# Two more waits in GpSimd's loop: a product behind an output sum, a coupling behind a division

## Chip, cores and metric

The kernel runs on one core of a Trainium2 chip. The metric is device time in microseconds of one execution, taken as the median of several runs. The engines of the core are PE (TensorE, matrix products), DVE (VectorE), ACT (ScalarE), POOL (GpSimd) and SP (SyncE, which issues the transfers). Each runs its own list of instructions in order, and they meet in semaphores: an instruction that finishes raises a counter, and another engine waits until that counter has reached a value.

## What is computed

A decoder layer over 64 independent sequences of 256 tokens and 256 features. It is a state-space mixer, a cross-attention from the mixed tokens to a context of 120 tokens plus the tokens themselves, and a "coupled" feed-forward of three cycles, each followed by a residual layer norm.

```python
x = layernorm(x + mixer(x))            # SSD with chunks: C, B, decay matrix Lmat, x * dt
x = layernorm(x + xattn(ctx, x))       # 8 heads of 64, softmax over 120 + 256 keys
x = layernorm(x + ffn(x))

# mixer, the part that matters here
Y_diag = einsum('bclhn,bcshn,bhcls,bcshp->bclhp', C, B, Lmat, x)   # Lmat = exp(segsum(A)), masked

# ffn, the part that matters here
out = x
for _ in range(3):
    tf = coupling_net(out)             # four layers, one number per token
    coupling = 0.1 + range * (0.7 * gf + 0.3 * tf - 0.5) * 2.0
    out = out + coupling * twist(out)
```

## The kernel before

One sequence is a whole tile of work: 256 tokens are two tiles of 128 partitions. The kernel is written by hand for each engine. Every engine's program is a prologue, a loop `for p in range(2, NSEQ - 1)` with 61 turns and an epilogue, and each turn calls small functions for three sequences that are at different stages: `m + 1 = p + 1` enters the mixer, `a = p - 1` is in attention, `f = p - 2` is in the feed-forward. The order of calls in the loop bodies is the order on the engine; nothing reorders it. Waits are written by hand with `wait_ge`, which leaves out a wait that the engine has already passed.

The names that matter, with their lines:

- `times_g(s, q)` (POOL, L2136): one of four products per sequence, `Lm` times `G`, in place. `Lm` holds the decay matrices of eight heads, 384 columns each, and one product takes two heads, 768 columns. `G` is the product of C and B, written by ACT (L908). ACT makes the decays in `Lm` (L915 and L916, two instructions a head). PE uses the result in `y_pair` (L325), DVE takes that up in `y_out` (L1556).
- `masked(s, q)` (POOL, L2126): masks two heads of `Lm`.
- `factors(f)` (POOL, L2204 to L2219): turns the couplings of the three cycles into three factors per token, `of_x`, `of_tw`, `of_minus`. The coupling of the third cycle enters at L2208, from `t_col`, which ACT writes at L1029. Ten small instructions follow each other, the last is L2219; the last raise of `l_fac` is what `out_sum` waits for.
- `out_sum(f, i)` (DVE, L1738, L1740, L1741): an output tile of 128 tokens from `x2` and the three factors; three instructions, each raises `d_out[i]`. The loop sums tile 1 first, then tile 0.
- `out_stats`, `out_norm(f, i)` (DVE, L1421, L1424, L1430): the last layer norm, with the reciprocal root from POOL's `ffn(f, i)` (L2115, L2117) in between.
- `divide(a, d)` (DVE, L1666): the division of attention's heads, for heads 0 to 3 (d = 0) and 4 to 7 (d = 1); it raises `d_o`. It waits for `invT`, which comes by a transfer.
- `x2_raw(a, i)` (DVE, L1676) frees the bank of PSUM that `turn` (PE, L438) takes next, and `y_out` frees the one that `ctxT` (PE, L360) takes.
- `top` (DVE, L1638) is the row maximum of the scores that ACT's `exp` (L979) needs, `v_out` (ACT, L969) copies values that PE has made.

In POOL's loop the piece in question is:

```python
masked(m + 1, 2)
factors(f)
times_g(m + 1, 0)
masked(m + 1, 3)
times_g(m + 1, 1)
ffn(f, 1)
ffn(f, 0)
times_g(m + 1, 2)
```

Of the kernel before, what the change touches and what calls it, by code (L numbers as in the profile page):

```python
# [34 lines left out]
def decoder_layer(nc, x, xT, ctx_in, par_in, w_in, w_out, wq, wkv, wo, cw1, cw2, cw3, cw4, gw1, gw2, gw3, out):  # L35
# [25 lines left out]
    with es:  # L61
# [3 lines left out]
        def sems(*names):  # L65
            return [es.enter_context(nc.semaphore(n)) for n in names]
# [3 lines left out]
        def prm(name, i=0, rows=slice(0, P)):  # L70
# [135 lines left out]
        d_max, d_inv, d_tn, d_o, d_x2p, d_x2, d_base = sems(  # L206
            "d_max", "d_inv", "d_tn", "d_o", "d_x2p", "d_x2", "d_base")

        d_att, (d_f,), d_ffn = sems("d_att0", "d_att1"), sems("d_f"), sems("d_ffn0", "d_ffn1")
        d_out = sems("d_out0", "d_out1")  # L210
# [12 lines left out]
        def live(s):  # L223
            return 0 <= s < NSEQ
# [3 lines left out]
        def _(e):  # L228
# [213 lines left out]
            def values(s, c):  # L442
                if not live(s):
                    return
                b = bank_of["val", s, c] = take(ring_b)
                pe.wait_ge(a_v, 3 * s + 3)
                pe.wait_ge(a_tn, 8 * s + 2 * c + 2)
                pe.wait_ge(d_tn, 8 * s + 2 * c + 2)
                for j, (_, m) in enumerate(JT):
                    for k in range(2):  # L450
                        h = 2 * c + k
                        t = mm(banks[b][k * HD:(k + 1) * HD, 0:L], V[0:m, j, h * HD:(h + 1) * HD],  # L452
                               probT[0:m, (8 * s + h) % HP, j, :], start=j == 0, stop=j == len(JT) - 1)
                t.then_inc(p_val, 1)
                freed[b] = [(a_o, 4 * s + c + 1)]
# [956 lines left out]
        def _(e):  # L1412
# [3 lines left out]
            def norm(s, name, src, rows, done, pool_done, first=0):  # L1416

                stats, mv, _, rs = stat[name]
                n, each = len(src), 3 * len(src)
                for k, a_ in enumerate(src):  # L1420
                    e.bn_stats(stats[0:rows, first + k, :], a_).then_inc(done, 1)  # L1421
                ve.wait_ge(done, each * s + n)
                for k in range(n):
                    e.bn_aggr(mv[0:rows, first + k, :], stats[0:rows, first + k, :]).then_inc(done, 1)  # L1424
# [681 lines left out]
        def _(e):  # L2106
            po = Engine(e)
# [11 lines left out]
            def masked(s, q):  # L2119

                if not live(s):
                    return
                po.wait_ge(cum_in, 32 * s + 32)
                for c0 in (0, L):
                    pair = Lm[:, 2 * q:2 * q + 2, c0:c0 + P]
                    t = e.affine_select(out=pair, in_=pair, compare_op=ALU.is_ge, fill=MINUS, base=0, pattern=[[0, 2], [1, P]],  # L2126
                                        channel_multiplier=-1)
                t.then_inc(l_mask, 1)

            def times_g(s, q):  # L2130
                if not live(s):
                    return
                pair = Lm[:, 2 * q:2 * q + 2, :]
                po.wait_ge(a_dec, 8 * s + 2 * q + 2)
                po.wait_ge(a_G, s + 1)
                tt(pair, pair, G[:, :].unsqueeze(1).broadcast_to([P, 2, TRI]), ALU.mult).then_inc(l_Lm, 1)  # L2136

            def gated(s, q):
                if not live(s):
                    return  # L2140
                po.wait_ge(d_yD, 4 * s + q + 1)
                po.wait_ge(d_gate, 2 * s + 2)
                po.wait_ge(p_out, s)
                po.wait_ge(a_sq, 4 * s)
                tt(g[:, q, :], yD[:, q, :], gate[:, q, :], ALU.mult).then_inc(l_g, 1)

            def squares(s):
                if not live(s):
                    return
                po.wait_ge(a_sq, 4 * s + 4)  # L2150
                tt(sq[:, 0:2, :], sq[:, 0:2, :], sq[:, 2:4, :], ALU.add).then_inc(l_sum, 1)
                po.wait_ge(l_sum, 2 * s + 1)
                tt(sq[:, 0, :], sq[:, 0, :], sq[:, 1, :], ALU.add).then_inc(l_sum, 1)

            def inv_rms(s):
                if not live(s):
                    return
                po.wait_ge(d_msv, s + 1)
                po.wait_ge(d_x1p, 2 * s)
                tt(rms[:, :], ms[:, :], minus_half[:, 0:TT], ALU.pow).then_inc(l_rms, 1)  # L2160

            def mix(s):

                if not live(s):
                    return
                _, mv, ve_, rs = stat["mix"]
                po.wait_ge(d_mix, 8 * s + 4)
                ts(ve_[:, 0:TT], mv[:, :, 1], EPS, None, ALU.add).then_inc(l_mix, 1)
                ts(ve_[:, TT:2 * TT], mv[:, :, 1], 1.0 + EPS, EPS * EPS, ALU.mult, ALU.add).then_inc(l_mix, 1)
                po.wait_ge(l_mix, 3 * s + 2)  # L2170
                tt(rs[:, :], ve_[:, :], minus_half[:, :], ALU.pow).then_inc(l_mix, 1)  # L2171

            def context(s):
                if live(s):
                    rstd(s, "ctx", 1, J, d_ctx, l_ctx)

            def att(s, i):
                if live(s):
                    rstd(s, "att", 1, P, d_att[i], l_att[i], first=i)

            def ffn(s, i):
                if live(s):
                    rstd(s, "ffn", 1, P, d_ffn[i], l_ffn[i], first=i)

            def twist(s):

                if not live(s):
                    return
                po.wait_ge(d_f, FD * s + 3)
                tt(h_a[:, :, :], h_a[:, :, :], cpl[:, 0, :].unsqueeze(1).broadcast_to([P, KT, L]), ALU.mult).then_inc(l_tw, 1)  # L2190
                po.wait_ge(l_tw, 2 * s + 1)
                tt(h_b[:, :, :], h_b[:, :, :], h_a[:, :, :], ALU.subtract).then_inc(l_tw, 1)

            def factors(s):

                if not live(s):
                    return
                n = 8 * s
                po.wait_ge(d_out[0], 3 * s)
                po.wait_ge(d_out[1], 3 * s)  # L2200
                for k in range(2):
                    po.wait_ge(c_in[k], 16 * (s + 1))
                c, d, e_ = (c_col[:, k, :] for k in range(3))
                tt(cd[:, :], c, d, ALU.mult).then_inc(l_fac, 1)  # L2204
                tt(c_d[:, :], c, d, ALU.add).then_inc(l_fac, 1)
                po.wait_ge(d_base, s + 1)
                po.wait_ge(a_f, FA * s + 16)
                ts(e_, t_col[:, :], tf_gain[:, :], c_cyc[:, :], ALU.mult, ALU.add).then_inc(l_fac, 1)  # L2208
                po.wait_ge(l_fac, n + 3)
                ts(one_cd[:, :], cd[:, :], -1.0, 1.0, ALU.mult, ALU.add).then_inc(l_fac, 1)  # L2210
                tt(e_sum[:, :], e_, c_d[:, :], ALU.mult).then_inc(l_fac, 1)
                po.wait_ge(l_fac, n + 5)
                tt(e_one[:, :], e_, one_cd[:, :], ALU.mult).then_inc(l_fac, 1)
                po.wait_ge(l_fac, n + 6)
                tt(of_x[:, :], one_cd[:, :], e_sum[:, :], ALU.subtract)
                tt(of_tw[:, :], c_d[:, :], e_one[:, :], ALU.add).then_inc(l_fac, 1)
                po.wait_ge(l_fac, n + 7)
                ts(of_x[:, :], of_x[:, :], 1.0, None, ALU.add)
                ts(of_minus[:, :], of_tw[:, :], -1.0, None, ALU.mult).then_inc(l_fac, 1)  # L2219
# [25 lines left out]
            masked(0, 3)  # L2245
            context(1)
            times_g(0, 0)
            times_g(0, 1)
            times_g(0, 2)
            gated(0, 0)  # L2250
            times_g(0, 3)
# [37 lines left out]
            for p in range(2, NSEQ - 1):  # L2289
                f, a, m = p - 2, p - 1, p  # L2290
                squares(m)
                context(m + 1)
                inv_rms(m)
                mix(m)
                twist(f)
                masked(m + 1, 0)
                masked(m + 1, 1)
                masked(m + 1, 2)
                factors(f)
                times_g(m + 1, 0)  # L2300
                masked(m + 1, 3)
                times_g(m + 1, 1)
                ffn(f, 1)
                ffn(f, 0)
                times_g(m + 1, 2)
                times_g(m + 1, 3)
                gated(m + 1, 0)
                att(a, 0)
                att(a, 1)
                gated(m + 1, 1)  # L2310
                gated(m + 1, 2)
                gated(m + 1, 3)
# [11 lines left out]
            att(last, 0)  # L2324
            att(last, 1)
            factors(last - 1)
            twist(last)
            ffn(last - 1, 1)
# [228 lines left out]
```

## Time and profile before

| what | us |
|---|---|
| median of 3 runs | 3883.71 |
| range of the runs | 3880.34 to 3893.58 |
| the profiled execution's own time | 3894.0 |
| its span | 3892.2 |
| PE busy | 3802.1 (98%) |
| DVE busy | 3282.4 (84%) |
| ACT busy | 3241.6 (83%) |
| POOL busy | 1751.4 (45%) |

The profiled execution lies at the upper end of the runs, 10 us over their median. Times in the rows are us from the start of the span. A row of the timeline merges neighbours of one line and gives start, duration, engine, line and operation; what stands in brackets is how long the engine had been idle before it and what ended that. Records of neighbours on one engine overlap by up to some 0.09 us, since an instruction is taken up before the one ahead of it has ended. PE is busy all the time by this profile, so a change elsewhere counts when it makes PE wait.

### The profile page before, as it was taken

The numbers are of one execution on the slowest core, as the hardware profiler recorded it, in microseconds if no ns is written. First come the engines' busy times: TensorE is split into PE (matmuls) and PEld (weight loads), VectorE is DVE, ScalarE is ACT, GpSimd is POOL, SyncE is SP. The second block draws the span as 40 slices with busy tenths as digits, with TensorE's granted clock in tenths as the row PEclk, the third lists the DMA queues.
The fourth block names the chain that finished last, engine by engine and source line by source line (L and its number), as shares of the span: only waits on it lengthen the run. The fifth ranks groups of instructions, "written<-read, shape, count | busy, mean of one in ns | idle before, by whom it ended". The sixth has DMA issues, their size and how long they took to land.

```text
span 3892.2 us, 77180 instructions
## 1 busy us (share of the span) xinstructions
PE 3802.1 (98%) x25728; PEld 3004.2 (77%) x25728; DVE 3282.4 (84%) x8098; ACT 3241.6 (83%) x7812; POOL 1751.4 (45%) x2828
## 2 busy tenths in 40 slices
PE   6999999999999999999999999999999999999997
PEld 5777777877877777777778777777777777777775
DVE  7888888888888888888888888888888888888874
ACT  5788888888888888888888888888888888888885
POOL 3445444354454454443544544444535445444442
PEclk8999999999999999999999999999999999999998
DMA  3111112112111111121111111111211211111110
GB/s 96 54 56 49 54 44 61 54 42 59 56 44 54 55 50 54 44 61 54 42 58 57 44 54 48 57 54 44 61 51 45 57 54 48 54 46 59 54 38 17
DMA packets 312348, 203.13 MB, mean 52 GB/s; under 512 B 55056, under 2 KB 310928, under 8 KB 311952
## 3 DMA queue, kind: packets, MB, share of 16 engines
q1 hardware_dynamic: 311952, 198.20, 17.5%
q8 instruction: 206, 3.38, 0.4%
q14 instruction: 190, 1.56, 0.1%
HBM read 180.17 MB, written 17.96 MB: 51 GB/s over the span
## 4 chain that ended last, share of the span: by engine, by line
PE 59%; ACT 17%; DVE 16%; POOL 4%; issue 4%; DMA 1%; SPq 0%; DVEq 0%; POOLq 0%; ACTq 0%
PE psum L253 20%; PE psum L428 8%; PE psum L338 6%; PE psum L463 5%; PE psum L438 5%; PE psum L325 4%; PE psum L452 4%; ACT prob L979 3%; ACT h L1021 2%; ACT L979 2%; ACT L1021 2%; PE psum L497 2%; ACT xc L891 2%; POOL rs_mix L2171 2%; DVE nmax L1638 2%
## 5 line engine op out<-in xcount | busy, mean ns | idle before, releaser
L979 ACT ACTIVATE prob<-psum,nmax 128x376 f32<-128x376 f32 x1024 | 585.7, 576 | 40.1 <-DVE nmax L1638 36.7
L2136 POOL TENSOR_TENSOR Lm<-Lm,G 128x768 f32<-128x768 f32 x256 | 474.7, 1856 | 182.3 <-ACT Lm L916 127.1
L1638 DVE TENSOR_REDUCE nmax<-psum 128x1 f32<-128x376 f32 x1024 | 540.2, 538 | 14.9 <-PE psum L428 11.6
L438 PE MATMUL psum<-ident,prob 128*128 128x128 f32 (+1 forms) x3072 | 481.0, 276 | 8.7 <-DVE x L1676 6.6
L1442 DVE SCALAR_TENSOR_TENSOR u<-psum,par,u 128x253 f32<-128x253 f32 (+5 forms) x960 | 449.0, 479 | 26.6 <-ACT u L882 1.8
L428 PE MATMUL psum<-kT,q_sb 64*128 64x376 f32 x2048 | 470.5, 528 | 0.5 <-ACT prob L979 0.5
L438 PEld LDWEIGHTS psum<-ident,prob 128*128 128x128 f32 (+1 forms) x3072 | 363.5, 141 | 81.1 <-issue 43.9
L989 ACT ACTIVATE probT<-psum 128x384 f32<-128x384 f32 x512 | 253.0, 494 | 190.2 <-PE psum L438 189.9
L2126 POOL TENSOR_SCALAR_AFFINE_SELECT Lm<-Lm 128x256 f32<-128x256 f32 x512 | 205.8, 437 | 412.3 <-DMA Lm<-cum_row 412.3
L253 PE MATMUL psum<-x_hi,w_in_hi 128*128 128x256 f32 (+1 forms) x1152 | 358.6, 311 | 19.5 <-DVE w_in_lo L1764 9.3
L452 PE MATMUL psum<-probT,V 128*64 128x256 f32 (+1 forms) x3072 | 374.9, 385 | 0.3 <-ACT probT L989 0.3
L253 PE MATMUL psum<-x_hi,w_in_lo 128*128 128x256 f32 (+1 forms) x1152 | 326.3, 283 | 0.0
L253 PE MATMUL psum<-x_lo,w_in_hi 128*128 128x256 f32 (+1 forms) x1152 | 325.9, 283 | 0.0
L1657 DVE COPY probT<-psum 128x384 f32<-128x384 f32 x512 | 279.6, 546 | 42.9 <-PE psum L438 41.5
L452 PEld LDWEIGHTS psum<-probT,V 128*64 128x64 f32 (+1 forms) x3072 | 202.3, 136 | 134.8 <-ACT probT L989 33.1
L2190 POOL TENSOR_TENSOR h_a<-h_a,cpl 128x512 f32<-128x512 f32 x64 | 82.1, 1283 | 492.3 <-DVE h_pre L1724 492.3
L915 ACT ACTIVATE Lm<-Lm,ncum 128x256 f32<-128x256 f32 x512 | 262.2, 512 | 0.7 <-DVE ncum L1533 0.7
L463 PE MATMUL psum<-wo_sb,oT 128*128 128x256 f32 x1024 | 248.2, 385 | 0.7 <-DVE oT L1666 0.7
L979 ACT ACT_TABLE_LOAD x189 | 242.5, 1283 | 3.4
L253 PEld LDWEIGHTS psum<-x_hi,w_in_hi 128*128 128x128 f32 (+1 forms) x1152 | 215.1, 187 | 35.0 <-issue 20.1
L338 PE MATMUL psum<-w_out_sb,g 128*128 128x256 f32 x1024 | 237.3, 385 | 0.0
L463 PEld LDWEIGHTS psum<-wo_sb,oT 128*128 128x128 f32 x1024 | 188.9, 189 | 59.1 <-issue 33.0
(222 smaller groups left out, 11179.2 us busy)
## 6 DMA issues: line engine op xcount, KB each, us to landing
Lm<-cum_row SPq DMA_DIRECT2D x64, 1024.0 KB, 5.1
Lm<-cum_row SPq DMA_DIRECT2D x64, 512.0 KB, 6.5
invT<-inv_row SPq DMA_DIRECT2D x256, 128.0 KB, 3.0
xT_sb<-in_xT SPq DMA_DIRECT2D x64, 256.0 KB, 3.3
x_sb<-in_x SPq DMA_DIRECT2D x64, 256.0 KB, 3.6
result<-out_sb SPq DMA_DIRECT2D x64, 256.0 KB, 2.2
inv_row<-inv_t SPq DMA_DIRECT2D x512, 1.0 KB
ctx_sb<-in_ctx SPq DMA_DIRECT2D x64, 120.0 KB, 2.4
```

The lines of the kernel that those rows point to most:

```text
L253: t = mm(dst, a, b, start=n == 1, stop=n == 3 * KT)
L338: t = mm(banks[b][:, i * D:(i + 1) * D], g[:, c, i * P:(i + 1) * P], w_out_sb[:, c, :], start=c == 0, stop=c == CT - 1)
L428: mm(banks[b][:, 0:NK], q_sb[r, c, i * P:(i + 1) * P], kT[r, c, :], start=True, stop=True).then_inc(p_sc, 1)
L438: t = tr(banks[b][0:m, j * P:(j + 1) * P], prob[:, r, j0:j0 + m], ident[:, :])
L452: t = mm(banks[b][k * HD:(k + 1) * HD, 0:L], V[0:m, j, h * HD:(h + 1) * HD], probT[0:m, (8 * s + h) % HP, j, :], start=j == 0, stop=j == l ...
L463: t = mm(banks[b][:, 0:D], oT[:, c, i * P:(i + 1) * P], wo_sb[:, c, :], start=c == 0, stop=c == CT - 1)
L915: act(Lm[:, h, 0:L], Lm[:, h, 0:L], ACT.Exp, bias=ncum[:, 0, h:h + 1])
L979: act(prob[:, r, :], b[:, 0:NK], ACT.Exp, bias=nmax[:, n:n + 1], accum_out=psum_row[:, n:n + 1]).then_inc(a_exp, 1)
L1442: stt(u[0:rows, c, d:L], src[:, 0:L - d], prm("conv_w", 4 * c + 3 - d, slice(0, rows)), u[0:rows, c, d:L], ALU.mult, ALU.add).then_inc(don ...
L1638: e.tensor_reduce(nmax[:, n:n + 1], banks[bank_of["sc", s, n]][:, 0:NK], AX.X, ALU.max, negate=True).then_inc(d_max, 1)
L1657: cp(probT[:, (8 * s + 2 * c + k) % HP, :, i * P:(i + 1) * P], b[:, 0:len(JT) * P].rearrange("p (j t) -> p j t", j=len(JT))).then_inc(d_tn, 1)
L2136: tt(pair, pair, G[:, :].unsqueeze(1).broadcast_to([P, 2, TRI]), ALU.mult).then_inc(l_Lm, 1)
```

## The change

The function `times_g` gets an optional wait ahead of its own: until DVE has done all three instructions of `out_sum(f, 1)`. The loop gives it to the first product of a turn. The function `factors` gets one ahead of L2208: until DVE has done both divisions of sequence `a`. No instruction is added, removed or moved otherwise; prologue and epilogue call both functions without the new argument.

```diff
-            def times_g(s, q):
+            def times_g(s, q, summed=None):
+
                 if not live(s):
                     return
+                if summed is not None:
+                    po.wait_ge(d_out[1], 3 * summed + 3)
                 pair = Lm[:, 2 * q:2 * q + 2, :]
                 po.wait_ge(a_dec, 8 * s + 2 * q + 2)
                 po.wait_ge(a_G, s + 1)
...
-            def factors(s):
+            def factors(s, divided=None):
...
                 po.wait_ge(d_base, s + 1)
                 po.wait_ge(a_f, FA * s + 16)
+                if divided is not None:
+                    po.wait_ge(d_o, 2 * divided + 2)
                 ts(e_, t_col[:, :], tf_gain[:, :], c_cyc[:, :], ALU.mult, ALU.add).then_inc(l_fac, 1)
...
-                factors(f)
-                times_g(m + 1, 0)
+                factors(f, divided=a)
+                times_g(m + 1, 0, summed=f)
                 masked(m + 1, 3)
                 times_g(m + 1, 1)
```

POOL's list of instructions keeps its order and its length. Only what its instructions wait for changes. The piece from the last masks of a turn to its first product, with the semaphores that each instruction waits for, in the kernel before (`d_out` are raised by `out_sum`, `a_f` and `a_G` by ACT's L1029 and L908, `a_dec` by its decays):

```order
L2204 TENSOR_TENSOR cd<-c_col 128x2 [waits c_in0,c_in1,d_out1,d_out0]
L2205 TENSOR_TENSOR c_d<-c_col 128x2
L2208 TENSOR_SCALAR c_col<-t_col,tf_gain,c_cyc 128x2 [waits a_f,d_base]
L2210 TENSOR_SCALAR one_cd<-cd 128x2 [waits l_fac]
L2211 TENSOR_TENSOR e_sum<-c_col,c_d 128x2
L2213 TENSOR_TENSOR e_one<-c_col,one_cd 128x2 [waits l_fac]
L2215 TENSOR_TENSOR of_x<-one_cd,e_sum 128x2 [waits l_fac]
L2216 TENSOR_TENSOR of_tw<-c_d,e_one 128x2
L2218 TENSOR_SCALAR of_x<-of_x 128x2 [waits l_fac]
L2219 TENSOR_SCALAR of_minus<-of_tw 128x2
L2136 TENSOR_TENSOR Lm<-Lm,G 128x768 [waits a_G,a_dec]
```

The same piece of the changed kernel, whose lines have other numbers (L2214 is L2208 of before, L2139 is L2136):

```order
L2208 TENSOR_TENSOR cd<-c_col 128x2 [waits c_in1,c_in0,d_out0]
L2209 TENSOR_TENSOR c_d<-c_col 128x2
L2214 TENSOR_SCALAR c_col<-t_col,tf_gain,c_cyc 128x2 [waits d_o,a_f,d_base]
L2216 TENSOR_SCALAR one_cd<-cd 128x2 [waits l_fac]
L2217 TENSOR_TENSOR e_sum<-c_col,c_d 128x2
L2219 TENSOR_TENSOR e_one<-c_col,one_cd 128x2 [waits l_fac]
L2221 TENSOR_TENSOR of_x<-one_cd,e_sum 128x2 [waits l_fac]
L2222 TENSOR_TENSOR of_tw<-c_d,e_one 128x2
L2224 TENSOR_SCALAR of_x<-of_x 128x2 [waits l_fac]
L2225 TENSOR_SCALAR of_minus<-of_tw 128x2
L2139 TENSOR_TENSOR Lm<-Lm,G 128x768 [waits a_G,a_dec,d_out1]
```

No instruction moved. `d_o` is new at the third coupling, `d_out1` at the product, and the first factor's wait for `d_out1` is gone, because POOL has passed that value in the turn ahead.

## Rows read from the trace of the kernel before

**Rows 1.** The page, busy time, share of the span and count of each engine.
```profile
PE 3802.1 (98%) x25728; PEld 3004.2 (77%) x25728; DVE 3282.4 (84%) x8098; ACT 3241.6 (83%) x7812; POOL 1751.4 (45%) x2828
```

**Rows 2.** Windows, each one turn long: length, busy time of engines, granted clock.
```profile
core 0: us, PE busy (x) PEld busy (x) DVE busy (x) ACT busy (x) POOL busy (x), PEclk, DMA share, GB/s
1908.49:1967.55 59.06, 58.81 (x405) 46.59 (x404) 50.73 (x127) 50.49 (x123) 27.73 (x44) 1.00 0.18 53
779.66:840.97 61.31, 59.19 (x404) 46.85 (x404) 53.46 (x127) 50.62 (x123) 26.97 (x44) 1.00 0.17 51
657.66:720.58 62.92, 60.77 (x405) 47.76 (x404) 53.26 (x127) 50.75 (x123) 26.91 (x44) 0.97 0.17 49
```

**Rows 3.** Timeline of DVE in an ordinary turn: start, duration, instruction, idle before.
```profile
1908.56 0.69 DVE L1666 TENSOR_TENSOR oT<-oT,invT 128x512 f32<-128x512 f32 x1
...
1911.15 0.35 DVE L1738 TENSOR_SCALAR out_sb<-x,of_x 128x256 f32<-128x256 f32 x1 [0.84 <-POOL of_minus L2219]
...
1911.81 0.35 DVE L1741 SCALAR_TENSOR_TENSOR out_sb<-x,of_minus,out_sb 128x128 f32<-128x128 f32 x1
...
1919.40 0.41 DVE L1430 TENSOR_SCALAR out_sb<-out_sb,mv_ffn,rs_ffn 128x256 f32<-128x256 f32 x1 [0.46 <-POOL rs_ffn L2117]
1919.73 0.41 DVE L1676 TENSOR_TENSOR x<-psum,x 128x256 f32<-128x256 f32 x1
```

**Rows 4.** Timeline of POOL in the same turn.
```profile
1908.64 0.83 POOL L2208 TENSOR_SCALAR c_col<-t_col,tf_gain,c_cyc 128x2 f32<-128x2 f32 x1 [3.04 <-ACT t_col L1029]
...
1910.89 0.23 POOL L2219 TENSOR_SCALAR of_minus<-of_tw 128x2 f32<-128x2 f32 x1
1911.87 1.96 POOL L2136 TENSOR_TENSOR Lm<-Lm,G 128x768 f32<-128x768 f32 x1 [0.75 <-ACT G L908]
...
1915.68 1.83 POOL L2136 TENSOR_TENSOR Lm<-Lm,G 128x768 f32<-128x768 f32 x1 [1.08 <-ACT Lm L916]
...
1919.73 3.76 POOL L2136 TENSOR_TENSOR Lm<-Lm,G 128x768 f32<-128x768 f32 x2 [0.36 <-ACT Lm L916]
```

**Rows 5.** Timeline of ACT in the same turn.
```profile
1908.19 0.27 ACT L1029 ACTIVATE t_col<-psum,half_b 128x2 f32<-128x2 f32 x1
...
1912.65 0.57 ACT L979 ACTIVATE prob<-psum,nmax 128x376 f32<-128x376 f32 x1 [0.24 <-DVE nmax L1638]
...
1915.19 0.41 ACT L916 ACTIVATE Lm<-Lm,ncum 128x128 f32<-128x128 f32 x1
...
1917.81 0.60 ACT L969 ACTIVATE V<-psum 120x512 f32<-120x512 f32 x1 [1.04 <-PE psum L253]
```

**Rows 6.** Timeline of a longer turn, around the third instruction of `out_sum(f, 1)`.
```profile
782.98 1.98 DVE L1741 SCALAR_TENSOR_TENSOR out_sb<-x,of_minus,out_sb 128x128 f32<-128x128 f32 x1
783.01 1.81 POOL L2136 TENSOR_TENSOR Lm<-Lm,G 128x768 f32<-128x768 f32 x1 [0.72 <-ACT G L908]
```

**Rows 7.** Timeline of the same turn around `out_norm(f, 0)`.
```profile
792.14 3.64 POOL L2136 TENSOR_TENSOR Lm<-Lm,G 128x768 f32<-128x768 f32 x2
792.21 1.90 DVE L1430 TENSOR_SCALAR out_sb<-out_sb,mv_ffn,rs_ffn 128x256 f32<-128x256 f32 x1 [0.46 <-POOL rs_ffn L2117]
794.03 0.41 DVE L1676 TENSOR_TENSOR x<-psum,x 128x256 f32<-128x256 f32 x1
```

**Rows 8.** Timeline of PE in that turn.
```profile
794.50 0.54 PE L438 MATMUL psum<-ident,prob 128*120 128x128 f32 x3 [0.95 <-DVE x L1676]
796.02 0.43 PE L360 MATMUL psum<-ident,ctx_n 120*128 120x120 f32 x2 [0.98 <-DVE xc L1556]
```

**Rows 9.** Waits of PE, whole span: total us, times, longest.
```profile
PE psum L360 <- DVE xc L1556: 6.8, 7, 1.0
PE psum L438 <- DVE x L1676: 6.6, 7, 1.0
```

**Rows 10.** Durations by line, whole span: count, ns minimum/median/maximum.
```profile
L1741 DVE SCALAR_TENSOR_TENSOR out_sb<-x,of_minus,out_sb x128: 336/344/1984, 187.5 to 3886.5; 128x128 f32<-128x128 f32 x128
...
L1430 DVE TENSOR_SCALAR out_sb<-out_sb,mv_ffn,rs_ffn x128: 382/413/1907, 194.3 to 3889.2; 128x256 f32<-128x256 f32 x128
...
L2208 POOL TENSOR_SCALAR c_col<-t_col,tf_gain,c_cyc x64: 343/824/885, 184.4 to 3882.9; 128x2 f32<-128x2 f32 x64
```

**Rows 11.** Timeline of DVE in a turn whose second division waits for its transfer.
```profile
2208.88 0.69 DVE L1666 TENSOR_TENSOR oT<-oT,invT 128x512 f32<-128x512 f32 x1 [1.18 <-DMA invT<-inv_row]
```

## The prediction, written before the changed kernel ran

> **What bounds the kernel.** I read the page's busy times first, then the windows, one loop turn each, then PE's waits, and last the timelines of DVE, POOL and ACT in one turn. PE is busy for 98% of the span [rows 1], and in an ordinary turn for 58.81 of 59.06 us [rows 2]. So nothing that DVE or POOL save in an ordinary turn shortens it, and only what makes PE wait lengthens it. Some turns are longer: 61.31 us in one, 62.92 in another, there with a granted clock of 0.97 [rows 2]. PE's waits name the cause: it waited seven times for L1676 and seven times for L1556, about 1 us each [rows 9].
>
> The timeline of such a turn shows what comes ahead of these waits. The third instruction of `out_sum(f, 1)`, L1741, takes 1.98 us in place of its median 0.344, and it ends just behind POOL's first product, which ran 1.81 us beside it [rows 6, 10]. 9 us later the same happens to L1430 of `out_norm(f, 0)`: 1.90 in place of 0.413, beside the third product [rows 7, 10]. Then PE idles 0.95 and 0.98 us [rows 8]. So a DVE instruction that reads and writes only SBUF and a POOL product exclude each other for their whole length, and whoever asks late stands still. In an ordinary turn DVE is first by a hair: L1741 starts at 1911.81 and the product at 1911.87, and it is the product that grows, 1.96 against 1.83 for its next [rows 3, 4]. In the long turns the lead was smaller, 0.03 us in the one shown [rows 6]. I count seven long L1741 (1.95 to 1.98 us), always with a long L1430 behind them. The seven turns exceed 59.06 by 2.25 to 3.86 us [rows 2], by my sum over the starts of L1029 21.2 us in all.
>
> **Second wait, product behind the sum.** It removes the first collision for good: the product now starts after L1741. That gives back 21.2 us at most in this execution, the L1430 collision of those turns included, since it came from the first one's delay. What it adds: the product starts some 0.08 us after L1741's end (ACT's L916 ends at 1915.60, the product that waits for it starts at 1915.68 [rows 4, 5]) in place of 0.04 ahead of it. Without the other wait that is 1912.16 + 0.08 = 1912.24, against 1911.87. Queued behind it are `masked(m + 1, 3)` and the second product, and that one has 1.08 us of idle time before it [rows 4]. The cover is enough here, and with the other wait's shift as well. Cost: nothing on the path.
>
> **First wait, third coupling behind the division.** L2208 starts at 1908.64, 0.18 after L1029's end at 1908.46, and lies beside the second division, which ends at 1909.25 [rows 3 to 5]. Its 0.83 us are mostly exclusion too: alone it takes 0.343 [rows 10], and it ends at 1909.47, 0.22 after the division. The new wait holds it until the division's end, and then it has its start-up still to do. How long from the release to the start is not shown for this wait. Bounds: 0.08 us, the row where the instruction's only outstanding wait was released, and 0.18, L2208's own row, where several waits stood ahead of it [rows 4, 5]. I take 0.18, since it is the same instruction with the same kind of waits. It then starts at 1909.43, ends at 1909.77, and everything after it is late by 1909.77 - 1909.47 = 0.30 us (0.20 by the other bound; up to 0.33 for one more wait).
>
> Who feels the 0.30? Queued behind it on POOL are the other factors, the products and `ffn`. DVE already idles 0.84 us for the last factor [rows 3], so L1738, L1741 and all of DVE behind them move by 0.30. ACT had idled 0.24 us for DVE's next maximum [rows 5], so its exponentials and the decays of head 3 move by 0.30, and the second product with them, to 1915.98. The two `ffn` follow on POOL, and DVE's second L1430 comes 0.30 later, at 1919.70. PE itself does not feel 0.30 us here. But the third product does not move: it waits for decays that ACT makes after `v_out`, and there ACT had 1.04 us idle for PE [rows 5]. It starts at 1919.73 as before; POOL had 0.36 of idle before it [rows 4], and 0.06 are left.
>
> So the change takes away the close race at L1741 and makes another one. L1430 led the third product by 1919.73 - 1919.40 = 0.33 us. Now it leads by 0.03 (0.13 to 0.00 by the bounds). Who wins at 0.03? At L1741 a lead of 0.03 lost and 0.06 won [rows 3, 4, 6]. L1430 needs more, as it takes longer from its recorded start to the port: a blocked L1741 ended 784.96 - 784.82 = 0.14 after the product, so of its free 0.35 the first 0.21 are start-up; for the blocked L1430, which ended at 794.11, half of the 3.64 gives the product's end as 793.96, so 0.15, and a start-up of 0.26. The lead it needs is 0.03 to 0.06 plus 0.05, some 0.08 to 0.11. **POOL wins, in nearly every turn.**
>
> **What a lost race costs.** In the long turn L1430 ended 1.97 us after the third product's start [rows 7]. From 1919.73 that is 1921.70, against 1919.81 now: DVE is 1.89 us late. The seven turns say what reaches PE. From L1741 to L1676 there are 11.05 us in the long turn and 7.92 in the ordinary one [rows 3, 6, 7], so DVE was 3.13 late, and the turn was 2.25 longer [rows 2]: 0.88 are covered. 1.89 - 0.88 = 1.01 us per turn. It falls on L360, the wait for L1556. Of the wait for L1676 little or nothing is left: 3.13 us late cost PE 0.95 there [rows 8], so about 2.2 are covered, more than 1.89. 61 turns by 1.01 are 61.6 us.
>
> **The sum**, against the profiled execution's own 3894.0 (10 over the median of the runs; the number of long turns explains such a spread, and the changed kernel has none of chance): 3894.0 - 21.2 + 61.6 = 3934.4, so **3935 us**, 1.3% over the median. For 0.85 to 1.25 us per turn it is 3925 to 3950. If idle PE time drops the granted clock, as in the 62.92 us turn (1.6 us more than the 61.31 one, at 0.97 [rows 2]), in one turn of ten, 10 us come on top.
>
> **Rivals.** (A) DVE keeps the third race. The condition is a lead above what L1430 needs, so a release as fast as 0.08, or a smaller start-up than I take. Then only the gain is left, 3894.0 - 21.2 = 3872.8, plus a few turns whose second division is late: one ends at 2209.57 [rows 11], over 1 us later than usual in its turn, and now the whole chain behind L2208 comes after it. I count six such turns, at some 1 us each for the worst: 3877, on the other side of my forecast or level with before. For it speaks that 0.03 is still a lead; against it, that L1741 lost with it. The Trainium skill, "SBUF — State Buffer", section "SBUF: two separate sides", says that the port pair of VectorE and GpSimd is an exclusive lock and that the one which starts first keeps it for its whole instruction. Read by recorded starts, it would give L1430 the port and this rival; [rows 6] disagree, where the instruction with the earlier start stood still.
>
> (B) The race goes either way, as it did at L1741, since the third product's start varies by some 0.03 us between turns. At one half: 3872.8 + 31 = 3904.
>
> (C) DVE's lateness is covered. 1.89 us would have to be under what PE can spare; then 3873. Against it are the seven waits for L1556, and the 0.88.
>
> (D) The waits hold nothing. The division ends 0.79 us after L1029 and L1741 ends after G is there in the ordinary turn, so both bind in each turn. I give this nothing.
>
> **Chances.** Forecast 0.62 (3925 to 3955), B 0.14 (3885 to 3925), A and C 0.20 (3868 to 3885), anything else 0.04. A measurement of this kernel can tell about 0.3% (12 us) from no change. Faster than 3872: a good half of A and C, and little besides, 0.13. Within 12 us: the rest of A and the low end of B, 0.14. Slower: 0.73. With the forecast and B alone only 0.76 are held, so the range has to reach A: 3870 to 3958. The likeliest case's own is 3925 to 3955.
>
> **What the changed profile would show.** L1741: no long one left. L2208: 0.34 us, starting 0.18 after the division. L1738 of tile 1: idle 1.1 in place of 0.84. L1430 of `out_norm(f, 0)`: some 60 of 1.9 us. PE's wait for L1556 at L360: some 60 times about 0.9; DVE busy time up by 61 by 1.5 less seven by 3.1, some 70 us. Turns of 60.1 us. I am wrong if L1430 keeps 0.41 (A), or if it is long and turns stay at 59.06 (C).

## The result and the profile after

The changed kernel takes 3941.0 us (median of 4 runs, 3939.28 to 3943.01) against 3882.4 for the kernel before in the same comparison. The ratio is 1.0144, with a 95% interval of 1.0126 to 1.0161: slower by 1.4%. The profiled execution took 3943.0 us, its span is 3940.9.

The page of the changed kernel, busy times of the engines, as in [rows 1]:

```profile
PE 3802.4 (96%) x25728; PEld 3001.7 (76%) x25728; DVE 3344.3 (85%) x8098; ACT 3249.1 (82%) x7812; POOL 1709.5 (43%) x2828
```

PE works as long as before, 3802.4 against 3802.1, in a span that is 48.7 us longer. DVE is busy 62 us longer and POOL 42 us shorter with the same instructions. So some instructions of DVE became longer, and PE idles more; the rows below show that it waits for DVE.

Two ordinary turns of the changed kernel as windows, to be held against [rows 2]:

```profile
core 0: us, PE busy (x) PEld busy (x) DVE busy (x) ACT busy (x) POOL busy (x), PEclk, DMA share, GB/s
1872.66:1932.72 60.06, 58.86 (x405) 46.57 (x404) 52.17 (x127) 50.71 (x123) 26.60 (x44) 1.00 0.18 52
2052.83:2112.87 60.04, 58.83 (x405) 46.56 (x404) 52.16 (x127) 50.69 (x123) 26.43 (x44) 1.00 0.18 52
```

The ordinary turn went from 59.06 to 60.06 us, with PE's work unchanged and the clock at its full level of 2.4 GHz in both.

Which instructions grew is told by durations by line over the whole span (count, ns minimum/median/maximum), as in [rows 10]:

```profile
L1741 DVE SCALAR_TENSOR_TENSOR out_sb<-x,of_minus,out_sb x128: 337/346/1414, 188.7 to 3935.1; 128x128 f32<-128x128 f32 x128
...
L1430 DVE TENSOR_SCALAR out_sb<-out_sb,mv_ffn,rs_ffn x128: 382/416/1973, 195.4 to 3937.9; 128x256 f32<-128x256 f32 x128
...
L2214 POOL TENSOR_SCALAR c_col<-t_col,tf_gain,c_cyc x64: 341/342/345, 186.0 to 3931.6; 128x2 f32<-128x2 f32 x64
```

The long L1741 of the loop are gone; the one of 1414 ns lies in the epilogue, where nothing was changed. L2214, the third coupling, never takes more than 0.345 us. L1430 is where the time went: of its 61 instances for tile 0 in the loop, 60 are long.

DVE in the turn that starts at 1872.66 (timeline: start, duration, instruction, idle before), to be held against [rows 3]:

```profile
1872.72 0.69 DVE L1666 TENSOR_TENSOR oT<-oT,invT 128x512 f32<-128x512 f32 x1
...
1875.64 0.35 DVE L1738 TENSOR_SCALAR out_sb<-x,of_x 128x256 f32<-128x256 f32 x1 [1.17 <-POOL of_minus L2225]
1876.30 0.35 DVE L1741 SCALAR_TENSOR_TENSOR out_sb<-x,of_minus,out_sb 128x128 f32<-128x128 f32 x1
...
1883.89 1.97 DVE L1430 TENSOR_SCALAR out_sb<-out_sb,mv_ffn,rs_ffn 128x256 f32<-128x256 f32 x1 [0.46 <-POOL rs_ffn L2117]
1885.78 0.41 DVE L1676 TENSOR_TENSOR x<-psum,x 128x256 f32<-128x256 f32 x1
```

POOL in the same turn, to be held against [rows 4]:

```profile
1873.63 0.34 POOL L2214 TENSOR_SCALAR c_col<-t_col,tf_gain,c_cyc 128x2 f32<-128x2 f32 x1 [2.97 <-DVE oT L1666]
1875.38 0.23 POOL L2225 TENSOR_SCALAR of_minus<-of_tw 128x2 f32<-128x2 f32 x1
1876.73 1.81 POOL L2139 TENSOR_TENSOR Lm<-Lm,G 128x768 f32<-128x768 f32 x1 [1.12 <-DVE out_sb L1741]
1880.17 1.84 POOL L2139 TENSOR_TENSOR Lm<-Lm,G 128x768 f32<-128x768 f32 x1 [0.86 <-ACT Lm L916]
1883.89 3.75 POOL L2139 TENSOR_TENSOR Lm<-Lm,G 128x768 f32<-128x768 f32 x2
```

The first product now starts 0.08 us behind L1741's end and meets nothing. The third product and L1430 both start at 1883.89: DVE's old lead of 0.33 us is used up, and DVE stands still until the product is done. By the trace's nanoseconds the product starts first in all 60 long turns, by 0.001 to 0.064 us.

PE's waits over the whole span (total us, times, longest), as in [rows 9]:

```profile
PE psum L360 <- DVE xc L1556: 58.7, 60, 1.0
```

That is the 1 us of every turn. Of the seven waits for L1676 one of 0.3 us is left.

One more line of DVE changed, L1438 (`x_lo`), which had a median of 1.037 us in the kernel before; it comes up again below:

```profile
L1438 DVE TENSOR_TENSOR x_lo<-xT_sb,x_hi x64: 680/789/1067, 5.3 to 3758.7; 128x512 fp32r<-128x512 f32 x64
```

### The profile page after: what moved, and what is told of

Its sections match the earlier page's. It is cut to its first block, busy times and chain, and to the rows that moved or that the text cites. A ratio compares the mean times of both kernels' runs of the same rounds, so it can differ in the third digit from the quotient of the medians.

```text
span 3940.9 us, 77119 instructions
## 1 busy us (share of the span) xinstructions
PE 3802.4 (96%) x25728; PEld 3001.7 (76%) x25728; DVE 3344.3 (85%) x8098; ACT 3249.1 (82%) x7812; POOL 1709.5 (43%) x2828
## 4 chain that ended last, share of the span: by engine, by line
PE 58%; ACT 17%; DVE 16%; issue 4%; POOL 3%; DMA 1%; SPq 0%; DVEq 0%; POOLq 0%; ACTq 0%
PE psum L253 20%; PE psum L428 8%; PE psum L338 6%; PE psum L463 5%; PE psum L438 5%; PE psum L325 4%; PE psum L452 4%; ACT prob L979 3%; ACT h L1021 2%; ACT L979 2%; ACT L1021 2%; PE psum L497 2%; ACT xc L891 2%; POOL rs_mix L2174 2%; DVE nmax L1638 2%
## 5 line engine op out<-in xcount | busy, mean ns | idle before, releaser
L2139 POOL TENSOR_TENSOR Lm<-Lm,G 128x768 f32<-128x768 f32 x256 | 466.8, 1824 | 152.5 <-ACT Lm L916 75.2
```

## Experiments

### Each wait alone

The output sum's wait alone, with `factors` as before:

```diff
-                factors(f, divided=a)
+                factors(f)
```

> Only the wait of the first product behind the output sum is kept, the one behind the division is taken out. My theory: the third race is lost only because the wait behind the division makes DVE 0.33 us late. Without it L1430 leads the third product by 0.33 us as before, L1741 no longer meets a product, so no long L1741, no long L1430, turns of 59.05 us, 3872 to 3877 us (0.2 to 0.3% under before). Rival 1, the wait behind the sum costs by itself, since the product starts later: turns over 59.3 and 3890 or more. Rival 2, the long L1430 has nothing to do with DVE's lateness: it stays long in most turns, about 3940.

Measured: 3871.5 us, ratio to the kernel before 0.9952 (0.9940 to 0.9965), so 0.5% faster. No L1741 and no L1430 of the loop is long. An ordinary turn of it as a window:

```profile
1956.30:2015.32 59.02, 58.78 (x403) 46.55 (x402) 50.95 (x127) 50.47 (x124) 26.90 (x44) 1.00 0.19 53
```

So this half of the change does what it should and costs PE nothing. It does shift one collision: the masks that follow the late product now begin together with L1738 of tile 0, whose median goes from 0.37 to 0.59 us:

```profile
1961.81 0.58 DVE L1738 TENSOR_SCALAR out_sb<-x,of_x 128x256 f32<-128x256 f32 x1
1961.84 0.82 POOL L2126 TENSOR_SCALAR_AFFINE_SELECT Lm<-Lm 128x256 f32<-128x256 f32 x2
```

DVE has made up these 0.22 us by the time of L1430. The time is 0.5 us under the range I gave for it. The runs of before in this comparison had a median of 3889.7 and a spread of 3884.7 to 3898.8, those of this kernel 3870.6 to 3872.9: with the race goes the spread as well.

The wait behind the division alone, with the first product as before:

```diff
-                times_g(m + 1, 0, summed=f)
+                times_g(m + 1, 0)
```

> Only the wait behind the division is kept. My theory: DVE comes 0.33 us later to the output sum while the first product still starts when G is there, so the first product takes the port in every turn: L1740 or L1741 of tile 1 is held for about 1.6 us in some 60 turns, L1430 of out_norm(f, 0) follows in the same turns, turns are 61.3 to 61.7 us as the seven long ones of before were, 4010 to 4035 us, up to 4060 if the clock drops as in some of those. Rival: the wait behind the division alone is what costs 1 us per turn, whatever the products do: about 3940.

Measured: 4064.9 us, 1.045 (1.0431 to 1.0469). DVE, then POOL, in one of its turns:

```profile
2056.42 0.35 DVE L1738 TENSOR_SCALAR out_sb<-x,of_x 128x256 f32<-128x256 f32 x1 [1.17 <-POOL of_minus L2225]
2056.80 1.93 DVE L1740 SCALAR_TENSOR_TENSOR out_sb<-x,of_tw,out_sb 128x128 f32<-128x128 f32 x1
...
2066.38 1.90 DVE L1430 TENSOR_SCALAR out_sb<-out_sb,mv_ffn,rs_ffn 128x256 f32<-128x256 f32 x1 [0.46 <-POOL rs_ffn L2117]
2068.20 0.41 DVE L1676 TENSOR_TENSOR x<-psum,x 128x256 f32<-128x256 f32 x1
```

```profile
2056.78 1.81 POOL L2139 TENSOR_TENSOR Lm<-Lm,G 128x768 f32<-128x768 f32 x1 [0.40 <-ACT G L908]
...
2066.31 3.63 POOL L2139 TENSOR_TENSOR Lm<-Lm,G 128x768 f32<-128x768 f32 x2
```

What chance did in seven turns of the kernel before happens here in all 61 of the loop, one instruction earlier (L1740, which started 0.02 us behind the product in the turn shown). It costs more than the change itself, though it holds one wait less: the wait behind the division makes DVE late, and the wait behind the sum had shielded one of the two places where lateness is punished. The rival, by which this wait costs 1 us whatever the products do, is out. PE waits for both of DVE's instructions, L1676 and L1556:

```profile
PE psum L360 <- DVE xc L1556: 58.6, 60, 1.0
PE psum L438 <- DVE x L1676: 56.7, 60, 1.0
```

Two of its turns as windows, a usual one and the one of the timelines:

```profile
1929.47:1991.18 61.71, 59.49 (x405) 46.83 (x404) 53.59 (x127) 50.67 (x123) 26.57 (x44) 1.00 0.17 51
2053.44:2116.74 63.30, 61.05 (x405) 47.92 (x404) 53.56 (x127) 50.68 (x123) 26.68 (x44) 0.97 0.17 49
```

Its time is 5 us over the 4060 that I had given as the end with a dropping clock. Of its 61 turns 36 take 61.5 to 62.0 us, where I had put the end at 61.7, and fifteen 63.2 to 64.3. The fifteen are those with a granted clock of 0.97, and at 1.6 us more than a usual turn they make up some 24 us.

### Closing the third race

The change plus a wait of the third product until DVE has written `out_norm(f, 0)`:

```diff
+                if normed is not None:
+                    po.wait_ge(d_ffn[0], 3 * normed + 3)
...
-                times_g(m + 1, 2)
+                times_g(m + 1, 2, normed=f)
```

> Both waits of the change, and a third one: the third product waits until DVE has written out_norm(f, 0). My theory: L1430 is back at 0.41 us in all turns, the third product starts at about 11.8 us after L1029's end in place of 11.26, which PE does not feel, turns are 59.05, 3873 to 3878 us. DVE is still 0.33 us late, so if lateness by itself costs anything it shows here. Rival, DVE's 0.33 us or the later products cost PE directly: turns between 59.3 and 60.1, 3890 to 3940.

Measured: 3862.3 us, 0.9928 (0.9915 to 0.9941). Same waits as the change, DVE 0.33 us late as in the change, the third product 0.5 us later, and the 1.4% loss is a 0.7% gain. PE's waits for L1556 are gone. So neither the late DVE nor the late products cost PE anything; the collision at L1430 was the whole loss. But the kernel is 11 us faster than I expected. Turns are not 59.05 but 58.83:

```profile
1951.89:2010.72 58.83, 58.59 (x404) 46.60 (x402) 50.50 (x127) 50.43 (x124) 26.62 (x44) 1.00 0.19 53
```

The same without the wait behind the division:

```diff
-                factors(f, divided=a)
+                factors(f)
```

> The product behind the sum and the third product behind out_norm(f, 0), without the wait behind the division: both races are closed and DVE is not made late. My theory: no long L1741 and no long L1430, 3872 to 3877, level with the sum alone, since the third race is won there anyhow. If turns with a late division lose the third race with the sum alone, this one is up to 5 us faster. Rival, more waits always cost: slower than the sum alone by 0.1% or more.

Measured: 3874.0 us, 0.9957 (0.9944 to 0.9970), no long L1741, no long L1430, and turns of 59.05. It is 2.5 us over the kernel with the sum's wait alone, 0.06%, with overlapping ranges of the runs, and not the gain of up to 5 us that I had thought possible: the third race was won there anyhow. So in the company of the other two, the wait behind the division gains 12 us. I had no reason for that.

### Where the other 0.2 us per turn come from

Laid side by side, the two last kernels' turns are the same on PE up to 18.8 us after L1029, where the products of `bcdt` come 0.24 us earlier in the faster one. `bcdt` is PE's first piece of the projections of a coming sequence. Its products need `x_lo` (DVE, L1438): the input is split into a high and a low part, and this instruction subtracts the high part from the input, both tensors of SBUF. DVE and POOL around it, first without and then with the wait behind the division:

```profile
1974.99 2.65 POOL L2150 TENSOR_TENSOR g<-xc,gate 128x256 f32<-128x256 f32 x3
1975.23 1.03 DVE L1438 TENSOR_TENSOR x_lo<-xT_sb,x_hi 128x512 fp32r<-128x512 f32 x1
```

```profile
1969.51 0.69 DVE L1438 TENSOR_TENSOR x_lo<-xT_sb,x_hi 128x512 fp32r<-128x512 f32 x1
1969.63 2.73 POOL L2150 TENSOR_TENSOR g<-xc,gate 128x256 f32<-128x256 f32 x3
```

Without the wait, POOL's gated products, which multiply the mixer's output by its gate (L2145 of the kernel before), start 0.24 us ahead of `x_lo` and hold it to 1.03 us; with it POOL's queue is late, `x_lo` starts 0.12 us ahead and takes 0.69. This is a fourth race, lost in nearly every turn of the kernel before (54 of its 64 L1438 take over 0.9 us, and the longest only 0.012 over the median), and it was not seen as a loss because it hardly varied. To test that, the kernel without the wait behind the division got a wait there:

```diff
-            def gated(s, q):
+            def gated(s, q, lowered=None):
                 if not live(s):
                     return
+                if lowered is not None and live(lowered):
+                    po.wait_ge(d_xlo, lowered + 1)
...
-                gated(m + 1, 1)
+                gated(m + 1, 1, lowered=m + 2)
```

> The output sum's wait and the third product's wait behind out_norm(f, 0), no wait behind the division, and a new one: POOL's second gated product (L2145) waits for DVE's x_lo (L1438). My theory on why both waits with the norm's (3862 us) beat the same without the division's (3874): there POOL comes 0.35 us later to the gated products and x_lo, which reads two tensors of SBUF, gets the port first (0.685 in place of 1.05 us), so PE's products that wait for it start 0.24 us earlier in every turn. Then this kernel has it too: L1438 0.685 in all turns, turns of 58.83 us, 3857 to 3863. Rival, the wait behind the division helps in another way, such as the coupling's shorter time: turns stay at 59.05 and 3872 to 3875.

Measured: 3860.7 us (3860.3 to 3861.3), 0.9946 (0.9933 to 0.9958) against the runs of before in this comparison. Durations of L1438, then an ordinary turn:

```profile
L1438 DVE TENSOR_TENSOR x_lo<-xT_sb,x_hi x64: 680/686/693, 5.2 to 3677.6; 128x512 fp32r<-128x512 f32 x64
```

```profile
1952.39:2011.23 58.84, 58.61 (x404) 46.60 (x403) 50.74 (x127) 50.45 (x123) 26.95 (x44) 1.00 0.18 53
```

That settles it: the gain of the wait behind the division in that company was `x_lo`'s place ahead of POOL. This kernel has the third coupling as before, under the division at 0.82 us, and loses nothing by it. Its median is the lowest of all here, 23.9 us under the kernel before in its own comparison and 80.3 under the changed kernel's, which was timed in another one. The 3862.3 above is of another comparison too, and its ratio to the kernel before is the lower of the two, so the 1.5 us between them are not shown to be a difference.

### How long a lead DVE needs, and what a shorter hold costs

The change with the division's wait written ahead of the two older ones:

```diff
+                if divided is not None:
+                    po.wait_ge(d_o, 2 * divided + 2)
                 po.wait_ge(d_base, s + 1)
                 po.wait_ge(a_f, FA * s + 16)
-                if divided is not None:
-                    po.wait_ge(d_o, 2 * divided + 2)
```

> The change with one thing different: in the third coupling the wait for the divisions is written ahead of the two older waits, so it is the one that the instruction itself carries. My theory: L2208's counterpart then starts about 0.09 us after the second division in place of 0.21, all behind it comes 0.12 us earlier, and L1430 leads the third product by about 0.11 us in place of the 0.02 to 0.04 that it now lacks. The lead that I worked out as needed is 0.08 to 0.11, so it should win in half of the turns or more: 3870 to 3905 us. Rival, 0.26 to 0.3 us are needed: long in nearly all turns, about 3935.

Measured: 3934.1 us, 1.0134 (1.0120 to 1.0148). The time is the rival's and not mine: I had the count of lost turns wrong. The lead needed is still mine and not the rival's 0.26 to 0.3. The third coupling does start earlier, 0.11 us behind the division in place of 0.21. Then L1430 leads the third product by 0.10 us at best, and by less where the product's own start comes early or the division late. In the loop's 61 turns, 54 L1430 are long and seven are not, one of these far from any race in the last turn. The six that won in a race had leads of 0.101 to 0.104 us; no lead of up to 0.094 won. A turn that won, at 0.11 by the rounded starts:

```profile
1217.71 0.41 DVE L1430 TENSOR_SCALAR out_sb<-out_sb,mv_ffn,rs_ffn 128x256 f32<-128x256 f32 x1 [0.46 <-POOL rs_ffn L2117]
1217.82 1.99 POOL L2139 TENSOR_TENSOR Lm<-Lm,G 128x768 f32<-128x768 f32 x1
```

Here it is the product that is stretched, 1.99 us. Of the windows of this turn and of one that lost, 0.08 us being its lead, only the second has the 1 us:

```profile
1206.62:1265.68 59.06, 58.86 (x405) 46.65 (x404) 50.93 (x126) 50.58 (x123) 27.19 (x44) 1.00 0.18 53
1805.38:1865.45 60.07, 58.87 (x405) 46.59 (x404) 52.31 (x127) 50.68 (x123) 26.93 (x44) 1.00 0.18 52
```

So the price of the race shows within one kernel, with the same waits. L1430 needs a lead of about 0.1 us by recorded starts. L1741 needed less: in the kernel before, its seven lost turns had leads of 0.000 to 0.029 us and its 53 won ones 0.026 or more.

The change with the third product cut into two instructions of one head each:

```diff
+                if split:
+                    for h in (2 * q, 2 * q + 1):
+                        t = tt(Lm[:, h, :], Lm[:, h, :], G[:, :], ALU.mult)
+                    t.then_inc(l_Lm, 1)
+                    return
...
-                times_g(m + 1, 2)
+                times_g(m + 1, 2, split=True)
```

> The change with the third product cut into two instructions of one head each (384 columns), the result is the same. My theory: L1430 still loses the race in nearly all turns, but is held for the first half alone, so it takes 1.0 to 1.1 us in place of 1.94; DVE is then 1.0 us late where 0.85 is covered, so turns are 59.1 to 59.3 us, 3875 to 3890 us. Rival 1, the lock is not given up between two instructions that follow closely: L1430 1.9 to 2.0 us and about 3941. Rival 2, what costs PE is not DVE's lateness but the 0.33 us on POOL and ACT: 3941 whatever L1430 takes.

Measured: 3890.5 us, 1.0018 (1.0007 to 1.0028). DVE, then POOL, in one turn:

```profile
1917.64 1.14 DVE L1430 TENSOR_SCALAR out_sb<-out_sb,mv_ffn,rs_ffn 128x256 f32<-128x256 f32 x1 [0.46 <-POOL rs_ffn L2117]
1918.71 0.41 DVE L1676 TENSOR_TENSOR x<-psum,x 128x256 f32<-128x256 f32 x1
```

```profile
1917.63 2.01 POOL L2141 TENSOR_TENSOR Lm<-Lm,G 128x384 f32<-128x384 f32 x2
```

```profile
PE psum L360 <- DVE xc L1556: 12.1, 60, 0.4
```

L1430 loses all the same, but is let in between the two halves and takes 1.14 in place of 1.97. PE's wait for L1556 falls from 58.7 to 12.1 us. The order and the waits are the change's. L360 starts 0.83 us earlier in the median turn than in the change, and 61 turns of that are the 50.6 us between the two kernels, so they are the length of the hold; `x_lo`, 0.69 us here in place of 0.79, brings 0.01 us a turn. The rival that a lock is kept between neighbouring instructions is out, and so is the one that POOL's or ACT's lateness costs PE. The turns are 59.2 us, and the time lies 0.5 us over the end of my range.

## Why the prediction was right, step by step

**The bound and the mechanism.** Right. Two more races, at L1430 and at `x_lo`, show the mechanism twice more, and each collision disappears with the order that keeps the two instructions apart.

**The second wait.** Right: worth some 18 us by itself (0.5%), at no cost. I had 21.2 for the profiled execution.

**The first wait.** The step with two bounds came out a little over the value I took: L2214 starts 0.21 us after the division's end (median; 1873.63 against 1873.41 in the turn shown), where I had 0.18 (the bounds were 0.08 and 0.18, with up to 0.03 more for one more wait). DVE's idle time for the last factor went from 0.84 to 1.17, so the shift is 0.33, not 0.30, and L1430's lead is 0.00 or less, not 0.03. It decided nothing: a lead of 0.1 would have been needed, and I had worked out 0.08 to 0.11. But it means that the changed kernel itself never put a lead of 0.03 to the test; the kernel with the division's wait written first did, and lost with leads from 0.015 on. That no unnoticed cost lay on the way is shown by the kernel with the third race closed. What I did not see is that the same lateness of POOL can help, at `x_lo`. In the change itself L1438 has a median of 0.789 in place of 1.037, and from L360 to L475, the stretch of PE's work that holds `bcdt`, the median turn takes 6.81 us in place of 6.96. So some 0.15 us of the loss in each turn are given back there.

**The race's price.** DVE's L1676 starts at 1885.78, 13.12 us after the turn's window begins, in place of 11.24: 1.88 late, where I had 1.89. Turns of 60.06 are 1.00 longer, where I had 1.01. The cover is then 0.88 again, as I had read from a long turn. It is not all slack, as I took it to be: PE's L360 is 1.18 us late, so 0.70 are slack, and the rest is mostly `x_lo`'s shorter time. It held because the long turn had that too: its L1438 took 0.784 us, and from L360 to L475 it took 6.78. That was luck. In the kernel with the division's wait alone the cover is about the same: L1676 at 14.76 is 3.52 late, the usual turn 2.70 longer, 0.82 covered.

**The sum.** 3894.0 - 21.2 + 61 by 1.0 gives 3934; the profiled execution took 3943. The rest lies mostly in irregular turns, by the starts of L1029: ten turns whose second division is late (the longest 61.39 us), some 5 us together, and four of about 61.1 us, some 4 us together. In the four, the window's waits of PE show, besides the usual wait at L360, one for `x_lo` of 0.7 to 0.9 us; the rows are of the turn at 1450.61, first PE's waits, then the timeline ahead of the second wait:

```profile
PE psum L360 <- DVE xc L1556: 1.0, 1, 1.0
PE psum L253 <- DVE x_lo L1438: 0.7, 1, 0.7
```

```profile
1468.81 0.63 ACT L849 ACTIVATE x_hi<-xT_sb 128x512 fp32r<-128x512 f32 x1 [0.92 <-DMA xT_sb<-in_xT]
1470.07 1.05 DVE L1438 TENSOR_TENSOR x_lo<-xT_sb,x_hi 128x512 fp32r<-128x512 f32 x1
```

In all four the transfer of the next input landed 0.5 to 0.9 us later than in the turn at 1872.66, by ACT's start on it, and `x_lo` then took 1.05 us beside the gated products. Why the transfer was late was not looked into. I had named late divisions only under the rival, and put no term for them or for such transfers into the forecast's sum. The clock did not drop in these turns (1.00 in each window that I read), so the 10 us that I had held ready for it stayed out. The kernel before had some 3 us of irregular turns besides its seven long ones, and the median turn is 60.09 us and not 60.06, some 2 us over the loop; with both, about 1 us of the 9 is left unexplained.

**The rivals.** A needed a lead that was not there; the kernel with the division's wait written first shows how near it was, and that the rule by which it would have come out, first start keeps the port, does not hold by recorded starts: L1430 lost 54 times, with starts 0.015 to 0.094 us ahead of the product. The Trainium skill, "SBUF — State Buffer", section "SBUF: two separate sides", names an exclusive lock held for a whole instruction. For the holding the traces agree, in both directions: L1430 1.97 us when POOL has it, the product 1.99 when DVE has it. B is out: where the leads run from -0.064 to -0.001, the product's small variation decides nothing. C is out, with PE's 60 waits. D, that the waits hold nothing, is out with the later starts of the coupling and the product. DVE's busy time rose by 62 us where I had some 70; L1438's time, 11 us less, and L1738's, 7 us more, were not in the sum.

## What to carry to other kernels

An order between VectorE and GpSimd that only timing keeps is a cost that a profile can show as chance: look for instructions whose maximum lies above their median by up to the length of another engine's instruction, and close each such race with a wait. A wait that closes one also moves all that stands behind it; so before it goes in, list for every pair of SBUF instructions behind it which engine leads and by how much, since moving one side by 0.3 us lost a lead of 0.33. And look at lines that are nearly always long, too: the race at `x_lo` had a maximum 0.012 us over its median, and winning it gave 12 us.

## What the runs showed of the hardware

The start that counts between VectorE and GpSimd is not the recorded one. L1741, which stands close behind another DVE instruction, lost with up to 0.029 us of lead and won from 0.026 on; L1430, which starts after a wait and reads two scalars from SBUF, lost with up to 0.094 and won from 0.101 on. That the start-up of an instruction makes this difference fits the durations, but no run varied it alone.

A semaphore wait had a price by its place. The third coupling starts 0.21 us after the division's end (median) when the division's wait is written behind two others, and 0.11 us when it is written first. By the records of both kernels the instruction itself carries the wait that is written first, and a separate semaphore instruction just ahead of it takes the other two. For a short start behind one late event, that event's wait was better written first here.

The granted clock stayed at 1.00 in the windows of the changed kernel, where PE idles about 1 us in a turn. In the kernel with the division's wait alone PE idles twice about 1 us within 2 us in each turn; the clock was 0.97 in fifteen of its 61 turns and 1.00 in the others. The 0.97 is one stretch of 3.4 us at the lower level of 1.2 GHz, 17 to 18 us behind the start of L1029, after PE has waited for L1676. The long turns of before show both as well: 1.00 in one and 0.97 in another [rows 2]. What decides between them is not shown.
